# Layer 2's odd 96 rows: 32 rows of up beside gate, the other 64 as fp32 products, x joined by GpSimd

## The chip, the cores and the metric

The kernel runs on one core of one Trainium2 chip. The metric is the device time of one execution in microseconds (us). The engines are called PE (TensorE), DVE (VectorE), ACT (ScalarE), POOL (GpSimd) and SP (SyncE, which issues most DMAs).

## The reference

1024 tokens of width 512 go through two layers in fp32. Layer 1 is attention-like: a small Taylor expansion over 128 channels plus a feed-forward of width 1248, added to the input and layer-normalised. Layer 2, where the change lies, is a feed-forward with weights that are quantised and dequantised in the kernel:

```python
dq1 = nf4_quant_dequant(w1)      # 1376 x 512, blocks of 64 along a row
dq2 = nf4_quant_dequant(w2)      # 1376 x 512
dq3 = nf4_quant_dequant(w3)      # 512 x 1376
gate = jnp.einsum('bsd,hd->bsh', x, dq1)
up = jnp.einsum('bsd,hd->bsh', x, dq2)
h = jax.nn.silu(gate) * up
return jnp.einsum('bsh,dh->bsd', h, dq3)
```

The result is added to x and layer-normalised again. `nf4_quant_dequant` divides each block by its largest magnitude, takes the nearest of 16 codes and multiplies back.

## The kernel before

**Products.** Nearly every fp32 operand is split into a high part and a low part of type fp32r, and a product is three matmuls (`product`, L1294 to L1297): high by high, high by low, low by high. x is in `x_hi` and `x_lo`, a weight chunk in one of two slots of `w_hi` and `w_lo`, a half of h in one of four slots of `l_hi` and `l_lo`.

**Layer 2, first stage.** w1 and w2 (gate and up) are taken 128 rows at a time, as eleven units (0 to 10); 1376 is ten times 128 and 96, so the last one, unit 10, has 96 rows of each. A pair is one unit with one half of the tokens (512): gate in one PSUM bank, up in the next, twelve matmuls of 512 columns for each (`pair`, L1337, `project`, L1307). There are 22 pairs, 0 to 21, on banks 0, 1 and 2, 3 in turn; pairs 20 and 21 are the odd ones. After a pair ACT writes silu of gate to h and copies up to `up2` (L682, L690), and POOL multiplies the two (L1257). A pair waits until ACT has copied the up of the pair but one before it; the copy waits for POOL's product of the pair but one before that.

**Layer 1's odd rows.** Layer 1's first chunk (pairs 0 and 1 there) has 96 rows too, and is already worked in another way: gate's 96 rows and 32 of up share one set of 128 columns of weights, and the other 64 rows of up are eight fp32 matmuls, not split, four for each token half, on 64 columns of weights (`project_up`, L1328 to L1335). They write rows 0 to 63 and 64 to 127 of one bank.

**Quantising.** Units 0 to 10 lie in `Q`; units 11 to 16 are w3, two chunks of it each (the last: one). A unit is worked in eight steps. Before them DVE takes the block maxima and POOL divides by them (L1211, by reciprocals). At step k (1 to 7; step 0 has no level) ACT draws a line into an int8 tile `side` (L599 from L640; step 0 is L637), POOL clamps it to a `level` (L1220), DVE adds it up in PSUM (L887; for k=1 L883, which reads `side` and `level`, both in SBUF). After step 7 DVE multiplies the maxima back (L890). I write 15.4 for step 4 of unit 15. There are four `side` and three `level` buffers. At 10.3 DVE also works out the scales of all of w3 (L868 to L872), for which ACT exchanges partners' maxima before 10.2; POOL's division of unit 11 comes before 10.5 and needs them.

**From a quantised unit to weights.** DVE transposes a unit into PSUM banks 4 and 5 (L1030), ACT copies the high part (`split_nf4`), DVE subtracts to get the low part (`lo_nf4`, L1039). A unit's first pair waits for both. Stage two (h by w3, jobs of twelve matmuls) does the same with chunks of w3 (L1047, L729, L1055), and its first job waits for chunk 0's low part.

**The order of the work** is written out: each engine runs its main list in order, and calls `beside()` ahead of each item, which does as many quantising steps as the next number of that engine's list in `SHARE` says (L222). Nothing on an engine overtakes what stands ahead of it. Around the places that matter the lists before read (main items by name, gate n for POOL's product of pair n):

```
POOL: 9.1 9.2 9.3 | gate 1 | gate 2 | 9.4 9.5 | gate 3 | 9.6 9.7 10.0 10.1 | gate 4 | 10.2 | gate 5 | 10.3 10.4 10.5 | gate 6 | 10.6 10.7 11.0 11.1 | gate 7 | 11.2 11.3 | gate 8
POOL: 15.0 to 15.3 | gate 19 | 15.4 15.5 | gate 20
DVE:  10.2 | low part of unit 4 | 10.3 | transpose of unit 5 | 10.4 to 11.1 | low part of unit 5
DVE:  14.7 15.0 to 15.4 | low part of w3 chunk 0 | transpose of chunk 2 | 15.5 | low part of chunk 1
```

Of the kernel before, what the change touches and what calls it, by code (L numbers as in the profile page):

```python
# [29 lines left out]
P = 128  # L30
# [11 lines left out]


REST, LEFT = F1 % P, 64
assert 2 * REST - P == LEFT
KEEP_FROM = 5
PRE0 = 2 * P

# [79 lines left out]

def unit_width(u):
    if u < C2:  # L130
        return 2 * DC * min(P, F2 - u * P)
    return D * min(2, C2 - 2 * (u - C2))


def w3_unit_of(c):
# [78 lines left out]
def multiplied(i, pool):  # L214
# [8 lines left out]
    "scalar": [  # L223
# [6 lines left out]
    "vector": [  # L230
# [5 lines left out]
    "gpsimd": [  # L236
# [3 lines left out]
}  # L240


# [18 lines left out]
def build(nc, xT, xN, w_pre, w_fuse, w_in, w_out, consts, w12, w3, w3_end, ident_in, out):  # L261
    with ExitStack() as ctx:  # L262
# [41 lines left out]
        def turned(f):  # L304

            return PS[:, XT_BANK:XT_BANK + 2, :].rearrange("p b n -> p (b n)")[:, 0:unit_width(f)]

        def term_tile(m, a):
            return (up if m == 0 else odd_term if m % 2 else even_term)[:, a, :]

# [61 lines left out]
        s_st, s_ln, s_sqrt, s_norm = sem("s_st"), sem("s_ln"), sem("s_sqrt"), sem("s_norm")  # L372
        s_norm_last, s_quarter, s_mean = sem("s_norm_last"), sem("s_quarter"), sem("s_mean")
        s_centred, s_root = sem("s_centred"), sem("s_root")
        s_xtr, s_turn, s_w3turn = sem("s_xtr"), sem("s_turn"), sem("s_w3turn")
        s_max3, s_other, s_max3_all = sem("s_max3"), sem("s_other"), sem("s_max3_all")
        s_max, s_floor, s_prep, s_nrm = sem("s_max"), sem("s_floor"), sem("s_prep"), sem("s_nrm")
# [60 lines left out]
        def h_half(n):  # L438

            i, (kind, c) = SEQ[n]  # L440
            a, layer = i % 2, 1 if kind == "out" else 2
            view = h[0:job_rows(SEQ[n][1]), c * TOK + a * HALF:c * TOK + (a + 1) * HALF]
            return view, (s_h, 2 * c + a + 1) if layer == 1 else product_made(PAIR2[c, a])

        def product_made(i):

# [9 lines left out]
            return f, half, 2 * ((i + 2) % 3) if layer == 1 else 2 * (i % 2)  # L456


        UP_BANK = 5

        def parted_up(i):

            _, half, bank = pair_of(1, i)
            return [(slice(LEFT, REST), PS[REST:P, bank, :]),
                    (slice(0, LEFT), PS[half * LEFT:(half + 1) * LEFT, UP_BANK, :])]

        def h_of(layer, i):
            f, half, _ = pair_of(layer, i)
            p = rows1(f) if layer == 1 else rows(f, F2)
            return h[0:p, f * TOK + half * HALF:f * TOK + (half + 1) * HALF]  # L470

# [52 lines left out]
        def _(sp):  # L524
# [15 lines left out]
                sp.dma_start(w_raw(j)[0:p, 0:n], src).then_inc(s_raw[j % RAW_SLOTS], 16)  # L540

            def load_unit(u):
                sp.dma_start(unit_read(u), w12[:, u * UW:u * UW + unit_width(u)]).then_inc(s_q[u], 16)

            def load_residual(a):

# [50 lines left out]
        def _(act):  # L597
# [76 lines left out]
            def silu(layer, i):  # L674
                beside()
                act.wait_ge(s_pair, i + 1 + (2 * C1 if layer == 2 else 0))
                if layer == 2 and i == 0:

                    act.wait_ge(s_llo_h, 2 * C1)
                dst = h_of(layer, i)  # L680
                bank = pair_of(layer, i)[2]
                nc.scalar.activation(dst, PS[0:dst.shape[0], bank, :], ACT.Silu).then_inc(s_silu, 1)  # L682
                if layer == 2 and on_pool(i):
                    k = multiplied(i, True) - 1
                    if k == 0:
# [4 lines left out]
                    copy(up2[0:dst.shape[0], k % 2, :], PS[0:dst.shape[0], bank + 1, :]).then_inc(s_up2, 1)  # L690

            def root_of_variance(layer, g):
                beside()
# [21 lines left out]

            def split_nf4(f):
                beside()
                m = rows(f, F2)
                act.wait_ge(s_turn, f + 1)
                wait_nf4_slot(act, f)  # L720
                copy(in_slot(w_hi, f, 2 * DC * m), turned(f)).then_inc(s_whi4, 1)

            def split_w3(c):
                beside()
# [107 lines left out]
        def _(dve):  # L832
# [80 lines left out]
            def gate_times_up(layer, i):  # L913
                beside()
                dst = h_of(layer, i)
                dve.wait_ge(s_silu, i + 1 + (2 * C1 if layer == 2 else 0))
                if layer == 1 and i < 2:
                    for to, up_rows in parted_up(i):
# [113 lines left out]

            def lo_nf4(f):
                beside()
                m = rows(f, F2)
                n = 2 * DC * m
                dve.wait_ge(s_whi4, f + 1)
                wait_nf4_slot(dve, f)
                v.tensor_tensor(in_slot(w_lo, f, n), turned(f), in_slot(w_hi, f, n).bitcast(F32),  # L1039
                                ALU.subtract).then_inc(s_wlo4, 1)  # L1040

            def turn_w3(c):
                beside()
# [160 lines left out]
        def _(pool):  # L1204
# [37 lines left out]
            def lo_of_h(n):  # L1242
# [26 lines left out]
            for n in range(PASS_START[2]):  # L1269
# [21 lines left out]
        def _(pe):  # L1291
# [27 lines left out]
            def project_first(half, bank):  # L1319

                wh, wl = (in_slot(w, JOB["in", 0], DC * P).rearrange("p (c m) -> p c m", c=DC) for w in (w_hi, w_lo))
                for c in range(DC):
                    xs = slice(half * HALF, (half + 1) * HALF)
                    last = product(PS[:, bank, :], wh[:, c, :], wl[:, c, :], x_hi[:, c, xs], x_lo[:, c, xs], c == 0,
                                   c == DC - 1)
                return last

            def project_up():  # L1328

                w = w_raw(JOB["in", 0])[:, DC * P:2 * DC * REST].rearrange("p (c m) -> p c m", c=DC)  # L1330
                for c in range(DC):
                    for half in range(2):
                        last = t_.matmul(PS[half * LEFT:(half + 1) * LEFT, UP_BANK, :], w[:, c, :],  # L1333
                                         xT_raw[:, c, half * HALF:(half + 1) * HALF], start=c == 0, stop=c == DC - 1)
                return last  # L1335

            def pair(layer, i):  # L1337
                f, half, bank = pair_of(layer, i)
                m = rows1(f) if layer == 1 else rows(f, F2)
                if layer == 1:  # L1340
                    slot = JOB["in", f]
                    if half == 0:
# [8 lines left out]
                else:  # L1351
# [9 lines left out]
                if layer == 1 and i < 2:  # L1361
                    last = project_first(half, bank)
                    if half == 0:
                        last = project_up()
                    last.then_inc(s_pair, 1)
                    return
# [1 line left out]
                if (layer, i) == (2, 1):  # L1368
# [181 lines left out]
```

## Time and profile before

| | |
|---|---|
| median of 3 runs | 410.32 us (410.29 to 411.04) |
| the profiled execution | 410.1 us |
| its span, first to last instruction | 408.1 us |
| granted PE clock | 0.997 of 2.4 GHz |
| PE busy | 399.7 us, 98% of the span |
| DVE, ACT, POOL busy | 324.1, 266.9, 289.4 us |
| DMA | 26.42 MB, 18.8% of the DMA engines' time |

The time of an execution is the span and about 2 us around it. Busy time is summed over the instructions of an engine. A matmul's record is longer than its share of PE, since matmuls are pipelined: the distance from one start to the next is what it costs.

### The profile page before, as it was taken

Reading aid. Unit: us, or ns where it says so; the run is one execution under the profiler, and the core shown is the slowest. Engines: PE = TensorE matmul, PEld = TensorE weight load, DVE = VectorE, ACT = ScalarE, POOL = GpSimd, SP = SyncE. Lnnn points to the kernel's source line nnn. Section 1 sums busy time; section 2 is a strip of 40 time slices with the busy share of each in tenths; the row PEclk is TensorE's granted clock in tenths of the full one; section 3 lists DMA queues with packets and bytes.
Section 4 is the critical chain, followed back from the end, with each engine's and each line's share of the span. In section 5 each row is a group of like instructions: output and inputs, shape, how many; then the busy total and the mean of one; then the engine's idle time right before and its main releaser. Section 6 shows DMA issues by size and latency. Waiting matters only on the chain.

```text
span 408.1 us, 5343 instructions
## 1 busy us (share of the span) xinstructions
PE 399.7 (98%) x1762; PEld 326.0 (80%) x1762; DVE 324.1 (79%) x386; ACT 266.9 (65%) x372; POOL 289.4 (71%) x228
## 2 busy tenths in 40 slices
PE   8999999999999999999999999999999999999993
PEld 6767888888888888888888888888888877888872
DVE  4539889789789997999969799887789989926035
ACT  5574676686585837466955668887769777732613
POOL 0177998987977499737992465799999998954330
PEclk9999999999999999999999999999999999999998
DMA  8993101100103361003052000000000000000202
GB/s 269 405 408 135 53 22 50 28 26 0 53 26 104 101 214 65 27 0 104 1 177 102 0 2 0 0 2 0 2 2 0 2 0 0 2 1 0 104 0 103
DMA packets 10010, 26.42 MB, mean 65 GB/s; under 512 B 1248, under 2 KB 1632, under 8 KB 9728
## 3 DMA queue, kind: packets, MB, share of 16 engines
q1 hardware_dynamic: 9552, 25.30, 17.8%
q10 hardware_dynamic: 432, 0.79, 0.7%
q8 instruction: 14, 0.23, 0.2%
q14 instruction: 12, 0.10, 0.1%
HBM read 23.99 MB, written 2.10 MB: 64 GB/s over the span
## 4 chain that ended last, share of the span: by engine, by line
PE 95%; DVE 1%; POOL 1%; ACT 1%; issue 0%; POOLq 0%; DVEq 0%; ACTq 0%
PE PS L1295 31%; PE PS L1296 31%; PE PS L1297 31%; PE PS L1429 1%; PE PS L1333 1%; PE PS L1423 1%; POOL level L1220 1%; DVE h L919 0%; POOLq L262 0%; DVE PS L887 0%; PE PS L1438 0%; ACT side L637 0%; ACT side L599 0%; PE PS L1444 0%; PE PS L1441 0%
## 5 line engine op out<-in xcount | busy, mean ns | idle before, releaser
L1220 POOL TENSOR_SCALAR level<-side 128x1024 f32<-128x1024 int8 (+2 forms) x119 | 128.9, 1083 | 27.8 <-ACT side L599 15.5
L887 DVE TENSOR_TENSOR PS<-PS,level 128x1024 f32<-128x1024 f32 (+2 forms) x102 | 120.1, 1178 | 21.8 <-POOL level L1220 17.8
L1295 PE MATMUL PS<-x_hi,w_hi 128*128 128x512 f32 (+1 forms) x340 | 132.8, 391 | 0.3 <-DVE h L919 0.3
L1297 PE MATMUL PS<-x_hi,w_lo 128*128 128x512 f32 (+1 forms) x340 | 132.4, 390 | 0.0
L1296 PE MATMUL PS<-x_lo,w_hi 128*128 128x512 f32 (+1 forms) x340 | 132.4, 389 | 0.0
L599 ACT ACTIVATE side<-Q 128x1024 int8<-128x1024 f32 (+2 forms) x84 | 80.5, 998 | 21.5 <-DVE PS L883 17.8
L1250 POOL TENSOR_TENSOR l_lo<-h,l_hi 128x512 fp32r<-128x512 f32 (+1 forms) x42 | 57.3, 1373 | 26.5 <-ACT l_hi L599 25.8
L1295 PEld LDWEIGHTS PS<-x_hi,w_hi 128*128 128x128 f32 (+1 forms) x340 | 63.4, 187 | 15.2 <-issue 0.8
L1297 PEld LDWEIGHTS PS<-x_hi,w_lo 128*128 128x128 f32 (+1 forms) x340 | 63.4, 187 | 13.8
L1296 PEld LDWEIGHTS PS<-x_lo,w_hi 128*128 128x128 f32 (+1 forms) x340 | 63.4, 187 | 13.4
L1296 PE MATMUL PS<-x_lo,l_hi 128*128 128x512 f32 (+1 forms) x144 | 56.1, 389 | 0.0
L1295 PE MATMUL PS<-x_hi,l_hi 128*128 128x512 f32 (+1 forms) x144 | 56.1, 389 | 0.0
L1297 PE MATMUL PS<-x_hi,l_lo 128*128 128x512 f32 (+1 forms) x144 | 56.1, 389 | 0.0
L1239 POOL TENSOR_TENSOR w_lo<-raw,w_hi 128x1024 fp32r<-128x1024 f32 (+2 forms) x15 | 30.8, 2054 | 19.5 <-ACT w_hi L599 18.9
L682 ACT ACTIVATE h<-PS 128x512 f32<-128x512 f32 (+1 forms) x42 | 24.9, 593 | 29.6 <-PE PS L1297 26.4
L1257 POOL TENSOR_TENSOR h<-h,Q 128x512 f32<-128x512 f32 (+1 forms) x22 | 30.3, 1377 | 18.2 <-ACT Q L599 15.9
L599 ACT ACTIVATE l_hi<-h 128x512 fp32r<-128x512 f32 (+1 forms) x42 | 25.9, 626 | 25.3 <-PE PS L1297 25.3
L599 ACT ACTIVATE side<-raw 128x1024 int8<-128x1024 f32 x35 | 35.1, 1059 | 6.0 <-DVE PS L883 6.0
L1295 PE MATMUL PS<-w_hi,l_hi 128*128 128x512 f32 (+1 forms) x80 | 31.5, 394 | 0.2 <-POOL l_lo L1250 0.2
L1295 PEld LDWEIGHTS PS<-x_hi,l_hi 128*128 128x128 f32 (+1 forms) x144 | 27.0, 188 | 5.7
L1296 PEld LDWEIGHTS PS<-x_lo,l_hi 128*128 128x128 f32 (+1 forms) x144 | 27.0, 188 | 5.6
L1297 PEld LDWEIGHTS PS<-x_hi,l_lo 128*128 128x128 f32 (+1 forms) x144 | 27.0, 188 | 5.6
(104 smaller groups left out, 514.1 us busy)
## 6 DMA issues: line engine op xcount, KB each, us to landing
Q<-w SPq DMA_DIRECT2D x10, 512.0 KB, 13.8
raw<-w_in SPq DMA_DIRECT2D x9, 512.0 KB, 9.9
raw<-w_out SPq DMA_DIRECT2D x13, 256.0 KB, 2.8
raw<-w SPq DMA_DIRECT2D x5, 512.0 KB, 3.9
R<-xN SPq DMA_DIRECT2D x2, 1024.0 KB, 5.7
raw<-w_fuse SPq DMA_DIRECT2D x7, 256.0 KB, 2.6
out<-R SPq DMA_DIRECT2D x7, 256.0 KB, 2.0
h<-xT SPq DMA_DIRECT2D x2, 512.0 KB, 6.8
```

The source lines that it names most:

```text
L599: return nc.scalar.activation(dst, src, ACT.Copy, **kw)
L682: nc.scalar.activation(dst, PS[0:dst.shape[0], bank, :], ACT.Silu).then_inc(s_silu, 1)
L887: v.tensor_tensor(total, total, level_of(s), ALU.add).then_inc(s_add, 1)
L1220: g.tensor_scalar(level_of(s), side_of(s), LIMITS[k][1], LIMITS[k][0], ALU.min, ALU.max).then_inc(s_level, 1)
L1239: g.tensor_tensor(lo, w_raw(j)[0:p, 0:n], hi.bitcast(F32), ALU.subtract).then_inc(s_wlo_in if JOBS[j][0] == "in" else s_wlo, 1)
L1250: g.tensor_tensor(lo, view, hi.bitcast(F32), ALU.subtract).then_inc(s_llo_h, 1)
L1257: g.tensor_tensor(dst, dst, up2[0:dst.shape[0], k % 2, :], ALU.mult).then_inc(s_h2, 1)
L1295: t_.matmul(dst, a_hi, b_hi, start=start, stop=False)
L1296: t_.matmul(dst, a_hi, b_lo, start=False, stop=False)
L1297: return t_.matmul(dst, a_lo, b_hi, start=False, stop=stop)
L1333: last = t_.matmul(PS[half * LEFT:(half + 1) * LEFT, UP_BANK, :], w[:, c, :], xT_raw[:, c, half * HALF:(half + 1) * HALF], start=c == 0, s ...
L1423: last = t_.transpose(PS[:, XT_BANK + t % 2, c * P:(c + 1) * P], R[:, t, c * P:(c + 1) * P], ident[:])
```

## The change

The 96-row chunk of w1 and w2 moves from unit 10 to unit 4 (`ODD`), so pairs 8 and 9 are the odd ones; the other units keep 128 rows and their order (`CHUNK_OF`), and h keeps its place by chunk. In the odd pairs gate's 96 rows and up's last 32 form one set of 128 columns. Up's first 64 rows are copied by ACT out of PSUM as plain fp32 (`up2_raw`, into free columns of h), and multiplied as fp32 with `x2_raw`, which POOL makes from `x_hi + x_lo` in four additions of 128x1024 (`join_x`), ahead of its gates 2, 3, 4 and 5. These eight fp32 matmuls follow the split ones of pair 8, for both token halves, and write bank 1; pair 10, whose up goes to bank 1, also waits until ACT has copied the up of pair 9. ACT copies the up of an odd pair in two parts. The lists in `SHARE` are dealt anew from about unit 8's last steps on.

```diff
+ODD = 4
+CHUNK_OF = [*range(ODD), C2 - 1, *range(ODD, C2 - 1)]
 def unit_width(u):
     if u < C2:
-        return 2 * DC * min(P, F2 - u * P)
+        return 2 * DC * (REST if u == ODD else P)
...
+        x2_raw = h[:, 6 * TOK:(6 + DC) * TOK].rearrange("p (c t) -> p c t", c=DC)
+        up2_raw = h[:, 5 * TOK:5 * TOK + DC * LEFT].rearrange("p (s n) -> p s n", s=2)
...
+        UP_BANK = {1: 5, 2: 1}
...
+                    if is_odd(layer, i):
+                        for to, up_rows in parted_up(layer, i):
+                            last = copy(up2[to, k % 2, :], up_rows)
+                        last.then_inc(s_up2, 1)
...
+                if f == ODD:
+                    copy(up2_raw, odd_part(turned(f), 2 * P, 2 * (P + LEFT)))
+                    copy(odd_part(dst, 0, 2 * P), odd_part(turned(f), 0, 2 * P)).then_inc(s_whi4, 1)
...
+            def join_x(half, k):
+
+                pool.wait_ge(s_xl, X_PARTS + TILES * (half + 1))
+                x, hi, lo = (t[:, 2 * k:2 * k + 2, half * HALF:(half + 1) * HALF] for t in (x2_raw, x_hi, x_lo))
+                g.tensor_tensor(x, hi.bitcast(F32), lo.bitcast(F32), ALU.add).then_inc(s_x2raw, 1)
...
             for i in range(2 * C2):
+                if 2 <= i < 6:
+                    join_x(i // 2 - 1, i % 2)
                 if on_pool(i):
                     gate_times_up(i)
...
+            def project_up2():
+
+                w = up2_raw.rearrange("p s (k m) -> p k s m", k=2)
+                for c in range(DC):
+                    pe.wait_ge(s_x2raw, 3 + c // 2)
+                    for half in range(2):
+                        last = t_.matmul(PS[half * LEFT:(half + 1) * LEFT, UP_BANK[2], :], w[:, c // 2, c % 2, :],
+                                         x2_raw[:, c, half * HALF:(half + 1) * HALF], start=c == 0, stop=c == DC - 1)
                 return last
...
+                if is_odd(layer, i):
+                    last = project_odd(layer, slot, half, bank)
+                    if layer == 2 and half == 0:
+                        last = project_up2()
...
+                    if layer == 2 and i > 1 and is_odd(2, i - 2) and half == 0:
+
+                        pe.wait_ge(*bank_free(i - 1))
                     project(layer, slot, 1, half, bank + 1, m).then_inc(s_pair, 1)
```

Written out as above, the lists after read:

```
POOL: 9.1 9.2 9.3 | gate 1 | join | gate 2 | join | 9.4 to 9.7 | gate 3 | join | 10.0 10.1 | gate 4 | join | 10.2 10.3 | gate 5 | 10.4 10.5 10.6 | gate 6 | 10.7 | gate 7 | 11.0 to 11.3 | gate 8
POOL: 15.0 to 15.3 | gate 19 | 15.4 15.5 | gate 20
DVE:  9.7 10.0 to 10.3 | low part of unit 4 | 10.4 10.5 | transpose of unit 5 | 10.6 to 11.1 | low part of unit 5
DVE:  14.7 15.0 to 15.4 | low part of w3 chunk 0 | transpose of chunk 2 | low part of chunk 1 | transpose of chunk 3 | 15.5 | low part of chunk 2 | 15.6
```

## Rows read from the trace of the kernel before

**Rows 1.** The page: busy time by engine, and two rows of the 40 slices

```profile
PE 399.7 (98%) x1762; PEld 326.0 (80%) x1762; DVE 324.1 (79%) x386; ACT 266.9 (65%) x372; POOL 289.4 (71%) x228
...
PE   8999999999999999999999999999999999999993
...
POOL 0177998987977499737992465799999998954330
```

**Rows 2.** The page: the chain that ended last, by engine

```profile
PE 95%; DVE 1%; POOL 1%; ACT 1%; issue 0%; POOLq 0%; DVEq 0%; ACTq 0%
```

**Rows 3.** Timeline of PE: first matmul of pair 20, first of stage two

```profile
329.67 0.39 PE L1295 MATMUL PS<-x_hi,w_hi 128*96 128x512 f32 x1
...
340.75 0.39 PE L1295 MATMUL PS<-w_hi,l_hi 128*128 128x512 f32 x1
```

**Rows 4.** Timeline of ACT: silu after pairs 7 and 8, high parts of w3

```profile
264.59 0.60 ACT L682 ACTIVATE h<-PS 128x512 f32<-128x512 f32 x1 [0.79 <-PE PS L1297]
...
270.03 0.60 ACT L682 ACTIVATE h<-PS 128x512 f32<-128x512 f32 x1 [1.55 <-PE PS L1297]
...
336.38 1.08 ACT L599 ACTIVATE w_hi<-PS 128x512 fp32r<-128x512 f32 x2
```

**Rows 5.** The chain in order of time: layer 1's eight fp32 matmuls (16 records)

```profile
19.79 3.61 PE PS L1333 x16
```

**Rows 6.** Busy time in stretches; columns PE, PEld, DVE, ACT, POOL, then clock, DMA

```profile
235.60:260.00 24.40, 24.40 (x109) 20.24 (x108) 23.85 (x23) 19.70 (x34) 14.41 (x14) 1.00 0.00 1
260.00:336.00 76.00, 76.00 (x337) 62.13 (x336) 64.07 (x56) 59.20 (x77) 71.69 (x58) 1.00 0.00 1
```

**Rows 7.** Timeline of POOL, 238 to 272 us: start, us, what, [idle before]

```profile
238.61 1.30 POOL L1257 TENSOR_TENSOR h<-h,Q 128x512 f32<-128x512 f32 x1 [3.01 <-ACT Q L599]
240.41 1.04 POOL L1220 TENSOR_SCALAR level<-side 128x1024 f32<-128x1024 int8 x1 [0.50 <-ACT side L599]
241.54 1.47 POOL L1211 TENSOR_TENSOR Q<-Q,rcp 128x768 f32<-128x768 f32 x1
...
253.20 0.83 POOL L1220 TENSOR_SCALAR level<-side 128x768 f32<-128x768 int8 x1 [2.07 <-ACT side L599]
...
259.74 1.92 POOL L1211 TENSOR_TENSOR raw<-raw,Q 128x1024 f32<-128x1024 f32 x1 [1.48 <-DVE Q L872]
...
268.35 3.03 POOL L1220 TENSOR_SCALAR level<-side 128x1024 f32<-128x1024 int8 x2
```

**Rows 8.** Timeline of POOL in layer 1: subtractions of 128x1024

```profile
65.47 3.37 POOL L1239 TENSOR_TENSOR w_lo<-raw,w_hi 128x1024 fp32r<-128x1024 f32 x1
...
74.02 2.40 POOL L1239 TENSOR_TENSOR w_lo<-raw,w_hi 128x1024 fp32r<-128x1024 f32 x1
```

**Rows 9.** Timeline of DVE: additions that read two SBUF tiles

```profile
65.37 1.22 DVE L883 SCALAR_TENSOR_TENSOR PS<-side,level 128x1024 f32<-128x1024 int8 x1
...
235.94 1.22 DVE L883 SCALAR_TENSOR_TENSOR PS<-side,level 128x1024 f32<-128x1024 int8 x1
...
253.21 1.63 DVE L883 SCALAR_TENSOR_TENSOR PS<-side,level 128x768 f32<-128x768 int8 x1
```

**Rows 10.** Timeline of DVE: unit 4's low part, the scales of w3

```profile
254.94 0.97 DVE L887 TENSOR_TENSOR PS<-PS,level 128x768 f32<-128x768 f32 x1
255.82 1.21 DVE L1039 TENSOR_TENSOR w_lo<-PS,w_hi 128x1024 fp32r<-128x1024 f32 x1
256.95 0.59 DVE L868 TENSOR_TENSOR Q<-Q 128x176 f32<-128x176 f32 x1
...
258.40 1.25 DVE L872 RECIPROCAL Q<-Q 128x176 f32<-128x176 f32 x1
```

**Rows 11.** Timeline of POOL: the level of step 15.4

```profile
334.82 1.04 POOL L1220 TENSOR_SCALAR level<-side 128x1024 f32<-128x1024 int8 x1
```

**Rows 12.** Timeline of DVE: step 15.4, then w3 chunk 0's low part

```profile
335.89 1.23 DVE L887 TENSOR_TENSOR PS<-PS,level 128x1024 f32<-128x1024 f32 x1 [0.76 <-POOL level L1220]
337.04 0.68 DVE L1055 TENSOR_TENSOR w_lo<-PS,w_hi 128x512 fp32r<-128x512 f32 x1
```

More of the change, by code:

```diff
@@ L44 @@
 REST, LEFT = F1 % P, 64
-assert 2 * REST - P == LEFT
+assert F2 % P == REST and 2 * REST - P == LEFT
+ODD = 4
+CHUNK_OF = [*range(ODD), C2 - 1, *range(ODD, C2 - 1)]
 KEEP_FROM = 5
@@ L442, in h_half @@
             view = h[0:job_rows(SEQ[n][1]), c * TOK + a * HALF:c * TOK + (a + 1) * HALF]
-            return view, (s_h, 2 * c + a + 1) if layer == 1 else product_made(PAIR2[c, a])
+            return view, (s_h, 2 * c + a + 1) if layer == 1 else product_made(PAIR2[CHUNK_OF.index(c), a])
         def product_made(i):
@@ L456, in pair_of, with is_odd, parted_up @@
             return f, half, 2 * ((i + 2) % 3) if layer == 1 else 2 * (i % 2)
-        UP_BANK = 5
-        def parted_up(i):
-            _, half, bank = pair_of(1, i)
+        UP_BANK = {1: 5, 2: 1}
+        def is_odd(layer, i):
+            return pair_of(layer, i)[0] == (0 if layer == 1 else ODD)
+        def parted_up(layer, i):
+            _, half, bank = pair_of(layer, i)
             return [(slice(LEFT, REST), PS[REST:P, bank, :]),
-                    (slice(0, LEFT), PS[half * LEFT:(half + 1) * LEFT, UP_BANK, :])]
+                    (slice(0, LEFT), PS[half * LEFT:(half + 1) * LEFT, UP_BANK[layer], :])]
         def h_of(layer, i):
             f, half, _ = pair_of(layer, i)
+            if layer == 2:
+                f = CHUNK_OF[f]
             p = rows1(f) if layer == 1 else rows(f, F2)
@@ L689, in silu @@
                         act.wait_ge(s_h2, k - 1)
-                    copy(up2[0:dst.shape[0], k % 2, :], PS[0:dst.shape[0], bank + 1, :]).then_inc(s_up2, 1)
+                    if is_odd(layer, i):
+                        for to, up_rows in parted_up(layer, i):
+                            last = copy(up2[to, k % 2, :], up_rows)
+                        last.then_inc(s_up2, 1)
+                    else:
+                        copy(up2[0:dst.shape[0], k % 2, :], PS[0:dst.shape[0], bank + 1, :]).then_inc(s_up2, 1)
             def root_of_variance(layer, g):
@@ L717, in split_nf4 @@
                 beside()
-                m = rows(f, F2)
                 act.wait_ge(s_turn, f + 1)
                 wait_nf4_slot(act, f)
-                copy(in_slot(w_hi, f, 2 * DC * m), turned(f)).then_inc(s_whi4, 1)
+                dst = in_slot(w_hi, f, unit_width(f))
+                if f == ODD:
+                    copy(up2_raw, odd_part(turned(f), 2 * P, 2 * (P + LEFT)))
+                    copy(odd_part(dst, 0, 2 * P), odd_part(turned(f), 0, 2 * P)).then_inc(s_whi4, 1)
+                else:
+                    copy(dst, turned(f)).then_inc(s_whi4, 1)
             def split_w3(c):
@@ L916, in gate_times_up @@
                 dve.wait_ge(s_silu, i + 1 + (2 * C1 if layer == 2 else 0))
-                if layer == 1 and i < 2:
-                    for to, up_rows in parted_up(i):
+                if is_odd(layer, i):
+                    for to, up_rows in parted_up(layer, i):
                         last = v.tensor_tensor(dst[to, :], up_rows, dst[to, :], ALU.mult)
@@ L1034, in lo_nf4 @@
                 beside()
-                m = rows(f, F2)
-                n = 2 * DC * m
                 dve.wait_ge(s_whi4, f + 1)
                 wait_nf4_slot(dve, f)
-                v.tensor_tensor(in_slot(w_lo, f, n), turned(f), in_slot(w_hi, f, n).bitcast(F32),
-                                ALU.subtract).then_inc(s_wlo4, 1)
+                hi, lo = (in_slot(w, f, unit_width(f)) for w in (w_hi, w_lo))
+                if f == ODD:
+                    hi, lo, src = (odd_part(x, 0, 2 * P) for x in (hi, lo, turned(f)))
+                else:
+                    src = turned(f)
+                v.tensor_tensor(lo, src, hi.bitcast(F32), ALU.subtract).then_inc(s_wlo4, 1)
             def turn_w3(c):
@@ L1317, in project, with project_odd @@
                 return last
-            def project_first(half, bank):
-                wh, wl = (in_slot(w, JOB["in", 0], DC * P).rearrange("p (c m) -> p c m", c=DC) for w in (w_hi, w_lo))
+            def project_odd(layer, slot, half, bank):
+                if layer == 1:
+                    parts = (in_slot(w, slot, DC * P) for w in (w_hi, w_lo))
+                    wh, wl = (w.rearrange("p (c m) -> p c m", c=DC) for w in parts)
+                else:
+                    parts = (in_slot(w, slot, unit_width(ODD)) for w in (w_hi, w_lo))
+                    wh, wl = (odd_part(w, 0, 2 * P).rearrange("p s (k m) -> p k s m", k=2) for w in parts)
                 for c in range(DC):
+                    w_h, w_l = ((w[:, c, :] if layer == 1 else w[:, c // 2, c % 2, :]) for w in (wh, wl))
                     xs = slice(half * HALF, (half + 1) * HALF)
-                    last = product(PS[:, bank, :], wh[:, c, :], wl[:, c, :], x_hi[:, c, xs], x_lo[:, c, xs], c == 0,
-                                   c == DC - 1)
+                    last = product(PS[:, bank, :], w_h, w_l, x_hi[:, c, xs], x_lo[:, c, xs], c == 0, c == DC - 1)
+                return last
+            def project_up2():
[5 more added lines that the diff above has]
+                                         x2_raw[:, c, half * HALF:(half + 1) * HALF], start=c == 0, stop=c == DC - 1)
                 return last
@@ L1332, in project_up @@
                     for half in range(2):
-                        last = t_.matmul(PS[half * LEFT:(half + 1) * LEFT, UP_BANK, :], w[:, c, :],
+                        last = t_.matmul(PS[half * LEFT:(half + 1) * LEFT, UP_BANK[1], :], w[:, c, :],
                                          xT_raw[:, c, half * HALF:(half + 1) * HALF], start=c == 0, stop=c == DC - 1)
@@ L1338, in pair @@
                 f, half, bank = pair_of(layer, i)
-                m = rows1(f) if layer == 1 else rows(f, F2)
+                m = P
                 if layer == 1:
@@ L1360, in pair @@
                     pe.wait_ge(s_xl, X_PARTS + (TILES if half == 0 and i < 2 else TT))
-                if layer == 1 and i < 2:
-                    last = project_first(half, bank)
-                    if half == 0:
+                if is_odd(layer, i):
+                    last = project_odd(layer, slot, half, bank)
+                    if layer == 2 and half == 0:
+                        last = project_up2()
+                    elif half == 0:
                         last = project_up()
@@ L1512, in by_squares @@
         parts = []
-        for f in range(C2):
+        for f in CHUNK_OF:
             rows_ = [w[f * P:(f + 1) * P].reshape(-1, SQ, 2, DC, BLOCK) for w in ws]
+            if f == C2 - 1:
+                gate, up = rows_
+                parts += [x.transpose(3, 1, 2, 0, 4).reshape(P, -1)
+                          for x in (np.concatenate([gate, up[LEFT // SQ:]]), up[:LEFT // SQ])]
+                continue
             parts.append(np.stack(rows_).transpose(4, 2, 0, 3, 1, 5).reshape(P, -1))
```

7 lines of the change are left out of this document (6 added, 1 removed), and 16 rows, old and new, of the table SHARE.

## The prediction

> **What bounds the kernel now.** I read the page first: PE is busy 98% of the span and nearly every slice of its row is 9, while POOL, at 71% over all, stands at 9 in nearly all slices of layer 2's first stage [rows 1]. The chain that ended last is 95% PE [rows 2]. So what shortens PE's own work shortens the run, as long as no other engine comes late. The reader is to see two things: where PE's work shrinks, and which engine behind it has the least to spare. Timelines of PE and ACT give PE's prices [rows 3, 4], the chain in order of time that of the fp32 matmuls [rows 5]; the stretches and timelines behind them [rows 6 to 12] are about POOL and DVE, because it is the engine to which the change gives work, in the very stage where it is full: between 260 and 336 us it is busy 71.69 of 76.00 us, and its 58 instructions leave the rest as gaps of under 0.1 us [rows 6].
>
> **PE.** Pairs 20 and 21, the 96-row ones, take from 329.67 to 340.75, 11.08 us for 48 matmuls [rows 3]: a set of 96 columns costs no less than one of 128. A pair of full width takes 5.44 us, the distance of ACT's silus after pairs 7 and 8 [rows 4], so 24 matmuls cost 5.44 us. The odd pairs become 24 such matmuls and eight fp32 ones. Those were already run in layer 1, with the same shape: 3.61 us [rows 5]. New cost 5.44 + 3.61 = 9.05 us, gain 2.03 us. That is the most that the change can bring, for PE does nothing else less.
>
> The Trainium skill ("FP8 and Floating Point Precision", TensorE Precision Notes) says that a true fp32 matmul takes four passes through the array. The row shows less than that rule would give one after the other: 3.61 us is 16 times 0.226 us for eight matmuls, two passes' worth each. By the page's four the change would lose on PE; that is a rival below.
>
> **POOL, the price.** Four joins of 128x1024 with two full fp32 operands. No join is in the trace; the same form, the subtraction of a split at that size, takes 2.40 us alone [rows 8], the division of a unit, whose second operand is one number a block, 1.92 [rows 7]. The bounds are 1.9 and 3.4, the 3.37 us being the case that collides (below). I take 2.4, as both operands are full: 9.7 us with the gaps. Unit 10 is now 1024 wide instead of 768: seven levels at 1.04 instead of 0.83 and a division at 1.92 instead of 1.47 [rows 7] are 1.9 us. Unit 4 is cheaper by as much, but its steps lie far ahead, and POOL later waits for gate 0 anyway, so nothing comes back.
>
> Third, collisions. Where DVE's step 1 (L883), which reads two SBUF tiles, started just ahead of a POOL instruction, at 65.37 us, that one took 3.37 us instead of 2.40 [rows 8, 9]. At 253.21 DVE's took 1.63 us, for POOL had begun at 253.20 a level of 0.83 us and DVE's addition went on only after it [rows 7, 9]. One holds the other off. In the kernel before, the two such additions at 235.94 and 253.21 [rows 9] met a POOL that was about to be idle and cost it nothing. Now the first falls into a join, ends near 239.2 and takes 0.6 us from gate 2; the second reaches into the fourth join and takes 1.0. That is 1.6 us. From unit 11 on the collisions are in the rows already.
>
> **POOL, the cover.** From 235.60 to 260.00 it is busy 14.41 of 24.40 us [rows 6]; less the gaps between 14 instructions, 9.4 us are idle, 3.01 of them ahead of gate 2, 2.07 and 1.48 near the end [rows 7]. The joins fall there. About 0.8 us stays idle: from the first join's end, 238.0, to gate 2, which ACT's copy holds to 238.6, and 0.2 before unit 11 is divided. So POOL falls behind by 9.7 + 1.9 + 1.6 + 0.8 - 9.4 = **4.6 us**. Behind 260 us there is no gap to catch up in [rows 6], and up to step 15.4 both kernels have the same steps, gates and subtractions on POOL.
>
> **Where it meets PE.** Four places, in order.
> - Unit 4's low part now stands behind 10.3 on DVE, and 10.3 behind the scales of w3. By my working the fourth join ends at 258.9 and the level of 10.2 at 260.0; its addition ends at 261.2, the scales take 2.7 (256.95 to 259.65) [rows 10], 10.3 another 1.1, the low part of 512 columns 0.7: 265.7. PE wants it at the end of pair 7, 264.6 [rows 4]. Before, it followed 10.2 at 255.82 [rows 10], over 7 us ahead. PE waits 1.1 us.
> - Unit 5's low part stands behind the level of 11.1, which now comes behind gate 7, at 272.9: ready at 275.3, wanted at 264.6 + 1.1 + 9.05 = 274.8. PE waits 0.5 us. From 275.3, twelve pairs at 5.44 end at 340.6, just before the 340.75 of before: these two waits alone eat most of the gain.
> - Units 6 to 10: before, their low parts came 5 us and more ahead of their pairs; POOL being 4.6 late and PE about level, they are close but in time.
> - Chunk 0 of w3. Its low part is behind 15.4 on DVE. The level of 15.4 ended at 335.86 [rows 11] and DVE had waited 0.76 us for it; the low part ended at 337.72 [rows 12], with ACT's high part done by then [rows 4], 3.0 us before PE wanted it [rows 3]. Now it ends at 337.72 + 4.6 = **342.3**, and stage two starts there: 342.3 - 340.75 = 1.6 us later than before.
>
> Behind that point: DVE needs about 1.8 us a chunk of w3 and PE 2.7, and unit 16 is small, so PE finds each chunk ready, if by little; I add nothing.
>
> **Costed at nothing, and why.** ACT's split of unit 4 in two copies and the second copies for the odd pairs (about 0.6 us each): ACT has 59.20 busy in 76 us [rows 6]. The wait of pair 10 on pair 9's copy: silu and two copies are 1.8 us, and the twelve gate matmuls of pair 10 ahead of the wait take 2.7; if ACT is held by a level, up to 1 us of it could show, and then the matmuls of up, nothing else, stand behind it. PE's wait for the joins: the last ends at 258.9, the fp32 matmuls come after 268. SP's queue moves nothing; the loads are the same bytes, long before.
>
> **Sum.** The profiled execution took 410.1 us: 410.1 + 1.6 = 411.7. The median shown is 0.2 above it, so 411.9 us.
>
> **Rivals.** What a measurement of this kernel can tell from no change is about 0.2%, 0.8 us.
> - *POOL late by 2.4 to 3.9 us only.* The collisions cost nothing (DVE gives way, or meets the idle that is left): 4.6 - 1.6 = 3.0, chunk 0 at 340.7, and PE's own path about there too: 410.3. For it: each collision depends on a few tenths. Against it: the two seen [rows 8, 9]. 27%.
> - *The joins are covered: faster.* If a join costs as little as the division, 1.92, and collides with nothing, POOL gets 7.7 + 1.9 against 9.4 of idle time, and is late by under 1 us. Below 1.0 us late, chunk 0 is ready by 338.7, where PE now arrives; then all of 2.03 us stays: 408.3. It decides at that one point, DVE's step 15.4. For it: 9.4 us of idle time stand in the very stretch where the joins are issued [rows 6]. Against it: 2.40 for the same form [rows 8]. 20%.
> - *The fp32 matmuls take twice as long here.* 7.2 us instead of 3.6: pair 10 starts 3.6 later, stage two at about 344, 413.5. Against it: the same shape in layer 1 [rows 5]. 4%.
> - *More waits than I see* (ACT held up by late gates and so late with lines, which makes POOL idle): 413 and over. 4%.
>
> My forecast has 45%: POOL late by 4.0 to 5.7 us, 411.2 to 413.0. The change not doing what it says is excluded as a rival: the 24 matmuls are gone from the code.
>
> **The numbers.** 411.9 us. The range takes in the middle rival, most of the faster one's partial cases (a gain of up to 1.6 us) and the slower ones to 413.4: 408.7 to 413.4. Faster by over 0.2%: 0.21, the covered case and a little. Within 0.2%: 0.28. Slower: 0.51, the forecast and the last two.
>
> **What would show it.** In the changed profile: eight fp32 matmuls in 3.6 us inside pair 8; joins of 2.4 us, one of them over 3; POOL without idle from 240 us on; gate 7 ending near 271.8; the level of 15.4 near 340.5; PE idle a little before pairs 8 and 10, and 1 to 2 us before the first matmul of stage two, put down to DVE. Wrong if joins take under 2 us, if POOL still shows idle time of some us before 260, or if stage two starts by 339.5.

## The result and the profile after

The changed kernel takes 412.17 us (median of 7 runs, 411.33 to 412.48), the kernel before 410.56 us in the same comparison: ratio 1.0032, 95% interval 1.0022 to 1.0042. It is slower by 1.6 us, as forecast (1.6 us on 410.3).

The page of the changed kernel, busy time, three rows of the slices and the chain:

```profile
span 410.5 us, 5334 instructions
...
PE 399.4 (97%) x1754; PEld 323.5 (79%) x1754; DVE 326.2 (79%) x386; ACT 267.8 (65%) x375; POOL 300.1 (73%) x232
...
PE   8999999999999999999999999899999999999993
...
POOL 0077998987876499737992599999999999874430
...
PE 93%; DMA 2%; DVE 1%; issue 1%; ACT 1%; POOL 1%; POOLq 0%; SPq 0%; DVEq 0%; ACTq 0%
```

POOL has 10.7 us more work than before [rows 1], and its row is full from the slice of 236 us on; PE's row has an 8 where it had nines. The chain has a DMA of the start in it: in this execution the first x came later, and everything up to layer 2 is 0.86 us later than before (ACT's silu of pair 2 starts at 238.25 instead of 237.39). In the profiled executions of this study, e5 and e6 apart, that silu lay from 0.2 us earlier to 1.4 us later than before, so times in layer 2 are compared after taking this shift off ("aligned"). That is also why the profiled execution, 412.5 us, is 2.4 us above the one of before and the medians are 1.6 apart.

The timeline of PE in the changed kernel: the start of pair 8, its fp32 matmuls, the start of pair 10 and of stage two. "issue" is a wait for which the view has no releaser; the low parts below end just ahead of them.

```profile
266.55 0.47 PE L1336 MATMUL PS<-x_hi,w_hi 128*128 128x512 f32 x1 [1.06 <-issue]
...
269.49 3.65 PE L1380 MATMUL PS<-h 128*64 128x512 f32 x16
...
277.28 0.47 PE L1336 MATMUL PS<-x_hi,w_hi 128*128 128x512 f32 x1 [1.19 <-issue]
...
343.12 0.47 PE L1336 MATMUL PS<-w_hi,l_hi 128*128 128x512 f32 x1 [0.26 <-issue]
```

Stage two starts at 343.12, aligned 342.26, 1.51 us after the 340.75 of before [rows 3]; I had put 1.6. PE stood idle only 0.4 us ahead of it, not the 1 to 2 us that I had named as a sign; the rest of the loss lies in the two waits before.

POOL's timeline: the joins are L1289, gate 2 is the L1296 at 239.48, the last row is the level of 15.4.

```profile
236.48 2.40 POOL L1289 TENSOR_TENSOR h<-x_hi,x_lo 128x1024 f32<-128x1024 f32 x1
239.48 1.64 POOL L1296 TENSOR_TENSOR h<-h,Q 128x512 f32<-128x512 f32 x1 [0.60 <-ACT Q L621]
241.07 2.41 POOL L1289 TENSOR_TENSOR h<-x_hi,x_lo 128x1024 f32<-128x1024 f32 x1
...
256.17 3.39 POOL L1289 TENSOR_TENSOR h<-x_hi,x_lo 128x1024 f32<-128x1024 f32 x1
...
340.12 1.04 POOL L1253 TENSOR_SCALAR level<-side 128x1024 f32<-128x1024 int8 x1
```

DVE's timeline: the two collisions with joins (L914, which was L883), the low parts of units 4 and 5 (L1073), 15.4 and chunk 0 of w3.

```profile
236.79 3.17 DVE L914 SCALAR_TENSOR_TENSOR PS<-side,level 128x1024 f32<-128x1024 int8 x1
...
255.66 1.65 DVE L914 SCALAR_TENSOR_TENSOR PS<-side,level 128x1024 f32<-128x1024 int8 x1
...
260.72 1.23 DVE L918 TENSOR_TENSOR PS<-PS,level 128x1024 f32<-128x1024 f32 x1 [3.42 <-POOL level L1253]
...
265.77 0.68 DVE L1073 TENSOR_TENSOR w_lo<-PS,w_hi 128x512 fp32r<-128x512 f32 x1
...
274.12 1.92 DVE L914 SCALAR_TENSOR_TENSOR PS<-side,level 128x1024 f32<-128x1024 int8 x1
275.96 1.21 DVE L1073 TENSOR_TENSOR w_lo<-PS,w_hi 128x1024 fp32r<-128x1024 f32 x1
...
341.20 1.23 DVE L918 TENSOR_TENSOR PS<-PS,level 128x1024 f32<-128x1024 f32 x1 [0.76 <-POOL level L1253]
342.34 0.68 DVE L1088 TENSOR_TENSOR w_lo<-PS,w_hi 128x512 fp32r<-128x512 f32 x1
```

The reader sees the whole mechanism here: DVE held by a join (3.17 us instead of 1.22), a join by DVE (3.39 instead of 2.40), 10.2's addition waiting 3.42 us for its level behind a join, and each low part ending just before PE's next start.

### The profile page after: what moved, and what is told of

It reads as the page before. It is cut to its first block, busy times and chain, and to the rows that moved or that the text cites. A ratio compares the mean times of both kernels' runs of the same rounds, so it can differ in the third digit from the quotient of the medians.

```text
span 410.5 us, 5334 instructions
## 1 busy us (share of the span) xinstructions
PE 399.4 (97%) x1754; PEld 323.5 (79%) x1754; DVE 326.2 (79%) x386; ACT 267.8 (65%) x375; POOL 300.1 (73%) x232
## 4 chain that ended last, share of the span: by engine, by line
PE 93%; DMA 2%; DVE 1%; issue 1%; ACT 1%; POOL 1%; POOLq 0%; SPq 0%; DVEq 0%; ACTq 0%
PE PS L1336 30%; PE PS L1337 30%; PE PS L1338 30%; DMA h<-xT 2%; PE PS L1389 1%; PE PS L1380 1%; PE PS L1484 1%; POOL level L1253 1%; DVE h L950 0%; POOLq L269 0%; DVE PS L918 0%; ACT side L659 0%; ACT side L621 0%; SPq L576 0%; ACT R L621 0%
## 5 line engine op out<-in xcount | busy, mean ns | idle before, releaser
L1336 PE MATMUL PS<-x_hi,w_hi 128*128 128x512 f32 x332 | 130.0, 392 | 2.7 <-issue 2.2
L1338 PE MATMUL PS<-x_hi,w_lo 128*128 128x512 f32 x332 | 129.3, 389 | 0.0
L1337 PE MATMUL PS<-x_lo,w_hi 128*128 128x512 f32 x332 | 129.2, 389 | 0.0
L1336 PEld LDWEIGHTS PS<-x_hi,w_hi 128*128 128x128 f32 x332 | 62.3, 188 | 19.1 <-issue 5.4
L1338 PEld LDWEIGHTS PS<-x_hi,w_lo 128*128 128x128 f32 x332 | 62.3, 188 | 13.1
L1337 PEld LDWEIGHTS PS<-x_lo,w_hi 128*128 128x128 f32 x332 | 62.3, 188 | 12.5
L1296 POOL TENSOR_TENSOR h<-h,Q 128x512 f32<-128x512 f32 (+1 forms) x22 | 29.8, 1356 | 14.6 <-ACT Q L621 13.1
```

The source lines that it names most:

```text
L1336: t_.matmul(dst, a_hi, b_hi, start=start, stop=False)
L1337: t_.matmul(dst, a_hi, b_lo, start=False, stop=False)
L1338: return t_.matmul(dst, a_lo, b_hi, start=False, stop=stop)
```

## The experiments

Ratios are to the kernel before, whose median lay between 410.4 and 410.7 us in these comparisons.

| run | median, us | ratio, 95% interval |
|---|---|---|
| e1, no joins | 408.75 | 0.9957 (0.9943 to 0.9970) |
| e2, two fp32 matmuls | 412.98 | 1.0058 (1.0038 to 1.0078) |
| e3, before with joins | 411.60 | 1.0027 (1.0017 to 1.0037) |
| e4, w3 first | 411.50 | 1.0027 (1.0017 to 1.0036) |
| e5, all joins early | 411.26 | 1.0014 (1.0005 to 1.0023) |
| e6, half of them early | 411.67 | 1.0029 (1.0018 to 1.0039) |
| e7, units 4 and 5 first | 415.83 | 1.0120 (1.0104 to 1.0136) |
| e8, these and w3 first | 415.41 | 1.0115 (1.0100 to 1.0130) |
| e9, joins behind the normalisation | 409.07 | 0.9966 (0.9953 to 0.9979) |
| e10, that and w3 first | 408.49 | 0.9957 (0.9943 to 0.9971) |
| e11, unit 4 first | 415.24 | 1.0107 (1.0090 to 1.0123) |

**e1: no joins.** In the changed kernel:

```diff
-                if 2 <= i < 6:
-                    join_x(i // 2 - 1, i % 2)
...
-                    pe.wait_ge(s_x2raw, 3 + c // 2)
...
-                                         x2_raw[:, c, half * HALF:(half + 1) * HALF], start=c == 0, stop=c == DC - 1)
+                                         x_hi[:, c, half * HALF:(half + 1) * HALF].bitcast(F32), start=c == 0, stop=c == DC - 1)
```

> The changed kernel without the four joins; the fp32 products read the high part of x alone, so the low part of x is left out of up's 64 rows. My theory (POOL falls behind by the joins and the collisions, and with it the low parts that PE waits for): POOL has only unit 10's extra 1.9 us, which 9.4 us of idle time cover; PE waits at pairs 8 and 10 and before stage two vanish, and PE's own saving of 1.7 to 2.0 us shows: 1.7 us below the kernel before (408.8 against 410.5). Rival (the new order on DVE, low parts behind the scales of w3 and behind more levels, makes them late, joins or not): still at or above the kernel before. Rival (the joins are only half of it): between, 0.5 us below to 0.5 above.

1.8 us below the kernel before. PE stands still at none of the three places; its timeline there, and POOL's level of 15.4:

```profile
267.30 0.39 PE L1336 MATMUL PS<-x_hi,w_lo 128*128 128x512 f32 x1
267.62 0.65 PE L1377 MATMUL PS<-x_hi,h 128*64 128x512 f32 x2
...
339.38 0.47 PE L1334 MATMUL PS<-w_hi,l_hi 128*128 128x512 f32 x1
```

```profile
336.38 1.05 POOL L1253 TENSOR_SCALAR level<-side 128x1024 f32<-128x1024 int8 x1
```

Stage two starts at 339.38, aligned 338.96, 1.8 us before that of before. The joins are the loss, all of it, and DVE's new order harms nothing without them. But POOL is not on time even here: the level of 15.4 ends at 337.43, aligned 337.0, 1.2 us later than before, where I had expected the idle time to cover all. At unit 11's division (260.62, aligned 260.2) it is 0.5 us late [rows 7], and at 273.29 it stood 0.5 us more ahead of a gate, for ACT. Chunk 0's low part ended at 339.28, just in time.

**e2: less work for PE.** Two fp32 matmuls instead of eight: `for c in range(DC)` is `for c in range(1)` in `project_up2`, with `start=True, stop=True`.

> The changed kernel with two fp32 matmuls instead of eight (three of the four parts of the sum over x are left out of up's 64 rows): 2.7 us of PE's work less. My theory: pair 10 waits for unit 5's low part, which POOL and DVE set at 277.2 us; pair 10 starts no earlier, and the time stays that of the changed kernel, 1.3 to 1.6 us above the kernel before; the idle time before pair 10 grows from 1.4 to about 4 us. Rival (PE's own work sets the end): 2.7 us less than the changed kernel, 1.1 us below the kernel before.

No gain from 2.7 us less of work. Pair 10 started at 277.89, aligned 276.5, as in the changed kernel (276.4), behind an idle time of 4.0 us; so the low part of unit 5 sets it. The time was even 0.8 us above the changed kernel's, for a reason that I had not expected. PE's timeline, and two stretches (the column behind the busy times is the granted clock):

```profile
277.89 0.47 PE L1336 MATMUL PS<-x_hi,w_hi 128*128 128x512 f32 x1 [3.81 <-DVE w_lo L1073]
...
280.74 0.63 PE L1336 MATMUL PS<-x_hi,w_hi 128*128 128x512 f32 x1
281.17 0.63 PE L1337 MATMUL PS<-x_lo,w_hi 128*128 128x512 f32 x1
```

```profile
280.00:285.00 5.00, 5.00 (x18) 4.01 (x17) 3.30 (x4) 3.83 (x5) 4.67 (x5) 0.74 0.00 0
285.00:290.00 5.00, 5.00 (x23) 4.13 (x23) 4.76 (x5) 4.76 (x7) 4.76 (x5) 1.00 0.00 0
```

From 279.5 to 282.5 us matmuls follow each other by 0.43 us instead of 0.23, and the granted clock of the stretch is 0.74: the lower level, 1.2 GHz. Some seven of them cost about 1.4 us. The one of six executions of this kernel with a mean clock of 0.998 took 411.5 us, the five with 0.987 to 0.992 took 412.6 to 414.3.

**e3: the joins alone.** The four `join_x` calls and their semaphore added to the kernel before, nothing else.

> The kernel before with the four joins alone added on POOL at the same places, their result unused. My theory: POOL falls behind by 9.7 + 1.6 + 0.8 - 9.4 = 2.7 us, the level of 15.4 ends at 338.6 instead of 335.9 and chunk 0's low part at 340.4, still 0.3 us ahead of PE: no change, within 0.3 us of the kernel before. Rival (the joins disturb PE by themselves, by reading x beside it): slower by 1 us or more, with longer matmuls. Rival (the collisions cost more than I take): slower by 0.5 us, with a wait before stage two.

1.0 us slower, where I had expected nothing. The mechanism is the one I had, its size and its reach are not. POOL's level of 15.4, and PE's second wait in stage two:

```profile
338.20 1.04 POOL L1223 TENSOR_SCALAR level<-side 128x1024 f32<-128x1024 int8 x1
```

```profile
343.33 0.50 PE L1306 MATMUL PS<-w_hi,l_hi 128*128 128x512 f32 x1 [0.50 <-ACT Q L602]
```

POOL is 3.4 us late (339.24 against 335.86 [rows 11]), not 2.7: the 1.48 us ahead of unit 11's division were not filled, 1.3 us more than I took, while the collisions took 0.8 us (gate 2 1.49 instead of 1.30, a level 1.42 instead of 0.83), not 1.6. Chunk 0's low part ended at 341.10; PE started stage two at 341.20, and then stood 0.7 us more, not for a low part but for ACT's copy of the last pair's up. That copy stands behind quantising lines on ACT, the first of which had waited 2.24 us for DVE, and DVE for POOL. PE also lost 0.2 us before one earlier matmul, at 313.60. No matmul was longer than before, so the joins don't disturb PE.

**e4: chunk 0 of w3 ahead of 15.4 on DVE.** Two numbers of DVE's list in `SHARE`, 6, 0 to 5, 1.

> The changed kernel with w3 chunk 0's low part ahead of step 15.4 on DVE, instead of behind it. In the changed kernel's trace the waits before pairs 8 and 10 alone bring PE to 342.7, and chunk 0's low part holds it to 343.1. My theory as now read: 0.4 us less than the changed kernel, 1.2 us above the kernel before. Rival (chunk 0's low part is what sets the time, as I had put it): 1.2 us less or more, level with the kernel before. A third: 15.4 and what follows it come later, and a later chunk waits: no gain.

Stage two at 342.16, aligned 341.82, 0.4 us earlier than in the changed kernel. The medians are 0.7 us apart, the ratios 0.2, and the intervals of the ratios overlap, so the size rests on the trace. By it chunk 0 was the last 0.4 us of the loss, and PE's own path, with the waits before pairs 8 and 10, set the rest.

**e5: all joins early.** In the changed kernel:

```diff
             def gate_times_up(i):
                 beside()
+                if i == 0:
+                    join_x(0, 0)
+                    join_x(0, 1)
...
-                if 2 <= i < 6:
-                    join_x(i // 2 - 1, i % 2)
+                if 2 <= i < 4:
+                    join_x(1, i % 2)
```

> The changed kernel with the joins at other places on POOL and nothing else: the two of the first token half just ahead of gate 0's wait, where POOL stands idle for 12.5 us, the two of the second half ahead of gates 2 and 3. My theory: two joins cost POOL nothing, the other two, unit 10's 1.9 us and one collision of 0.6 are 7.3 us against 9.4 us of idle time, so POOL is late by under 1 us; no wait before pairs 8 and 10 and stage two; 1.7 us below the kernel before, as without any join. Rival (a join costs by reading x beside PE, or the order of DVE's list costs): at least 0.7 us above that, at or over the kernel before.

0.6 us above the kernel before: wrong by 2.3 us. The waits before pairs 8 and 10 are gone. But earlier, two joins run at 218.07 to 222.83 us beside DVE's steps of layer 1's normalisation. POOL's and DVE's timelines:

```profile
218.07 4.76 POOL L1289 TENSOR_TENSOR h<-x_hi,x_lo 128x1024 f32<-128x1024 f32 x2
```

```profile
218.89 1.60 DVE L1015 TENSOR_SCALAR std<-mv 128x2 f32<-128x2 f32 x1
220.41 1.22 DVE L918 TENSOR_TENSOR PS<-PS,level 128x1024 f32<-128x1024 f32 x1
221.54 0.15 DVE L1018 RECIPROCAL std<-std 128x2 f32<-128x2 f32 x1
221.72 1.13 DVE L1019 TENSOR_TENSOR std<-std 128x2 f32<-128x2 f32 x1
```

In the changed kernel L1015 and L1019 take 0.17 and 0.16 us. Here each, on two elements a partition, ends with the join beside it (220.5 and 222.8). The two between them, an addition that has one operand in PSUM and a reciprocal, take their usual time beside the second join. The steps stand between PE and its next x, and PE waits twice:

```profile
230.55 1.23 PE L1487 MATMUL PS<-ident,R 128*128 128x128 f32 x8 [0.77 <-DVE x_lo L1049]
...
234.42 0.47 PE L1339 MATMUL PS<-x_hi,w_hi 128*128 128x512 f32 x1 [0.57 <-DVE x_lo L1049]
```

ACT's silu of pair 2 comes at 240.18, 1.9 us later than before once the 0.9 us are taken off by which it was already late at 216 us, ahead of the joins; with 0.3 us of wait ahead of stage two this is nearly all of the 2.3 us.

**e6: half of the joins early.** As e5, with the second token half's joins left ahead of gates 4 and 5.

> As the run before, but with the joins of the second token half left where the change has them, ahead of gates 4 and 5. My theory: 4.9 us of joins, 1.9 of unit 10 and a collision of 1.0 against the 6.4 us of idle time behind gate 2, of which some 1 us stays unfilled: POOL late by 2 us or a little more, half of the changed kernel's; between the two, 0.5 to 1.2 us below the kernel before. Rival (only the number of joins counts, not the idle time they fall in): the time of the changed kernel.

1.0 us above. It pays the same price in the normalisation (1.49 and 1.13 us for the same two operations) and keeps 0.6 us of wait before pair 10 and 0.4 before stage two. It says nothing against the theory, but it can't be read as support either; e5 and e9 do what it was meant to do.

**e7: units 4 and 5 ahead of levels on DVE.** In DVE's list 5, 2, 4, 0, 4 is now 4, 3, 2, 0, 6 (low part 4, transpose 5, low part 5, transpose 6, low part 6).

> The changed kernel with DVE's list put so that unit 4's low part comes ahead of step 10.3 and the scales of w3, and unit 5's ahead of steps 11.0 and 11.1. Both waits of PE there, 1.2 and 1.3 us, go. My theory: POOL is as late as before, so later low parts (unit 8's, w3 chunk 0's at 342) hold PE instead: 0.1 to 0.5 us less than the changed kernel. Rival (the waits before pairs 8 and 10 are the loss, POOL's lateness behind them is harmless): 2.5 us less than the changed kernel, 0.9 us below the kernel before.

5.1 us slower than before: my edit made a new wait. It put DVE's 11.1 behind unit 5's low part; ACT's line of 11.4 needs that addition, and ACT's copy of pair 9's up stands behind the line. That is the copy for which pair 10 now waits, on bank 1. ACT, then PE's two waits in pair 10, for unit 5's low part and on bank 1:

```profile
279.37 1.06 ACT L622 ACTIVATE side<-raw 128x1024 int8<-128x1024 f32 x1 [3.21 <-DVE PS L915]
```

```profile
275.93 0.47 PE L1337 MATMUL PS<-x_hi,w_hi 128*128 128x512 f32 x1 [1.48 <-DVE w_lo L1074]
...
282.18 0.50 PE L1337 MATMUL PS<-x_hi,w_hi 128*128 128x512 f32 x1 [3.25 <-ACT Q L622]
```

The wait that the change adds costs nothing where it is, and 3.4 us once ACT is held. The wait before pair 8 is gone, but that for unit 5's low part is still there, 1.6 us. The run doesn't test what it was made for. Part of the 5.1 us is the clock: the execution shown took 414.3 us at a mean clock of 0.998, the other four 415.6 to 416.3 at 0.990 to 0.994.

**e8: e7 and e4 together.**

> The run before and w3 chunk 0's low part ahead of step 15.4 as well. My theory: units 4 and 5 and chunk 0 are on time; unit 8's low part, behind 13.1, and ACT's copies, held behind lines that wait for POOL, are what is left: 0.8 to 1.5 us less than the changed kernel, level with the kernel before to 0.8 us above it. Rival (POOL's lateness costs only through these three low parts): 1.7 us below the kernel before, as without joins.

The same wait, 3.23 us, and 4.7 us slower than before. On the low parts nothing follows beyond e7. On the clock something does: PE stood idle equally long, 3.4 us, in both profiled executions, and behind it seven matmuls follow each other by 0.43 us here (282.6 to 285.6 us) and none in e7. The stretch from 280 to 285 us, e7 first, then e8:

```profile
280.00:285.00 5.00, 2.82 (x12) 2.35 (x13) 3.40 (x4) 4.94 (x8) 4.67 (x5) 1.00 0.00 0
```

```profile
280.00:285.00 5.00, 2.98 (x8) 2.38 (x9) 3.41 (x4) 4.94 (x8) 4.67 (x5) 0.75 0.00 0
```

**e9: the early joins behind the normalisation.** As e5, and one more wait ahead of the first two joins:

```diff
                 if i == 0:
+                    pool.wait_ge(s_shift, len(NORM_GROUPS))
                     join_x(0, 0)
```

> As the run with all joins early, but the two ahead of gate 0 also wait until DVE has finished layer 1's last normalisation (224.5 us), so that they run from there to 229.5. In the early run two small DVE operations of that normalisation, on 128x2 elements, took 1.60 and 1.13 us instead of 0.17 and 0.16 while a join ran on POOL, and PE waited 0.9 and 0.7 us for x. My theory: a POOL join holds off DVE, which hurts only where DVE is on PE's path; those 1.7 us come back and the rest of the early run's gain shows: 1.2 to 1.6 us below the kernel before. Rival (the joins held PE or ACT up, or the early run was slow for another reason): the time of the early run, 0.5 us above the kernel before.

1.3 us below the kernel before, 2.2 us below e5, with the same joins 6.6 us later. Its POOL and PE:

```profile
224.68 4.76 POOL L1289 TENSOR_TENSOR h<-x_hi,x_lo 128x1024 f32<-128x1024 f32 x2 [7.52 <-DVE std L1022]
229.66 1.30 POOL L1300 TENSOR_TENSOR h<-h,Q 128x512 f32<-128x512 f32 x1 [0.22 <-ACT Q L621]
```

```profile
339.31 0.47 PE L1340 MATMUL PS<-w_hi,l_hi 128*128 128x512 f32 x1
```

Both joins fit between the normalisation and gate 0, and PE doesn't wait before stage two but for 0.3 us.

**e10: e9 and e4 together.**

> The run before and, on DVE, w3 chunk 0's low part ahead of step 15.4. The early run still showed a wait of 0.3 us before stage two. My theory: that wait goes, 0.2 to 0.4 us less than the run before, so 1.5 to 1.9 us below the kernel before, near the time without any join. Rival (what follows 15.4 becomes late instead): no gain on the run before.

408.49 us, 1.9 us below the kernel before and 3.7 below the changed one (3.1 by the ratios): all of the saving on PE, with all of the work. Stage two starts at 338.86, aligned 339.06, 0.3 us earlier than in e9. That it beats e9 is not shown by the times: the ratios are 0.4 us apart and their intervals overlap.

**e11: unit 4 ahead of 10.3 only.** In DVE's list 5, 2 is 4, 3.

> The changed kernel with unit 4's low part ahead of step 10.3 and the scales of w3, and nothing else moved. My theory: the wait before pair 8 goes, but unit 5's low part comes when POOL and DVE let it, so pair 10 waits that much longer, 2.5 us instead of 1.3: the time of the changed kernel within 0.3 us, plus up to 1 us if PE's granted clock falls behind the longer idle time, as it did behind 4 us of it. Rival (each wait costs by itself): 1.2 us less than the changed kernel.

The wait before pair 8 went, as expected, and nothing was gained, as expected; but it is 3.1 us above the changed kernel, more than I allowed. PE's timeline and one stretch:

```profile
278.84 0.47 PE L1337 MATMUL PS<-x_hi,w_hi 128*128 128x512 f32 x1 [3.53 <-DVE w_lo L1074]
```

```profile
280.00:285.00 5.00, 5.00 (x18) 3.98 (x17) 3.68 (x4) 4.79 (x6) 4.75 (x4) 0.73 0.00 0
```

Pair 10 starts at 278.84, aligned 277.4, 1.0 us later than in the changed kernel (the scales of w3 come later on DVE, and with them unit 11's division). The two waits of 1.2 and 1.3 us have become one of 3.7, and behind it the clock falls again, for seven matmuls: 1.4 us. Against this stands the 0.4 us of wait ahead of stage two, which is gone; stage two starts 2.2 us later, aligned. The other 0.6 us between the two profiled executions (415.24 and 412.48) come from ahead of pair 2 (shifts of 1.43 and 0.86 us). The medians differ by 0.3 us more, since the changed kernel's profiled execution lies that much above its median.

## Why the prediction was right, point by point

- **PE's saving, 2.03 us.** The odd pairs took 9.4 us, not 9.05: 2.94 for the first twelve matmuls, 3.58 for the fp32 ones, 2.86 for the last. So 1.7 us. The fp32 matmuls cost what layer 1's do [rows 5]; what was missed is about 0.1 us at each change between kinds and after a wait. The size didn't enter the result, since pair 10 hung on unit 5's low part (e2). Four passes one after the other, the rival's 7.2 us, are ruled out: sixteen records in 3.6 us. Whether a matmul here takes fewer passes, or those on the two halves of the columns overlap, no run shows.
- **A join, 2.4 us.** 2.40 alone, 3.39 in collision [rows 8]. Right.
- **The collisions, 1.6 us.** 0.3 on gate 2 and 1.0 on the fourth join. Right but for 0.3.
- **POOL late by 4.6 us.** The level of 15.4 ends at 341.16, aligned 340.3: 4.4 us late [rows 11]. Right as a total, the parts less so. By e1, 3.3 us of it come from the joins and their collisions, by e3, 3.4 us; the rest is there without joins (e1: 0.5 us at unit 11's division, 1.2 at 15.4). My sum had POOL on time without joins, since it set 1.9 us of work against all 9.4 us of idle time.
- **Unit 4.** Its low part ended at aligned 265.6; I had 265.7. PE waited 1.2 us.
- **Unit 5.** Aligned 276.3; I had 275.3, so PE waited 1.3 instead of 0.5 us. The step that failed: I let DVE's addition of 11.1 start when its level was there, aligned 273.0 as I had put it (272.9), and take 1.2 us. DVE was still multiplying unit 10's maxima back (L921), 0.3 us; by then POOL had begun the next level, and the addition took 1.92 us, held off by it, 0.7 us: a collision in the other direction, which I had seen in the rows but costed only for POOL. It is not the joins' doing: without them (e1) the same addition takes 1.93 us.
- **Chunk 0 of w3 sets the time.** It ended at aligned 342.2, as I said (342.3). But PE's own path, 340.6 in my sum, was at 341.8 (e4), nearly all through unit 5's low part. So the loss of 1.5 us was set by the waits before pairs 8 and 10 up to its last 0.4 us, not by chunk 0 from 340.6 on. The number stood because both paths end near each other: e4 takes only the last part off, e11 only moves the first wait into the second. The total was right by the path that I had named; the share between the two paths was not, and that it didn't matter was luck: 0.5 us more on unit 5 and PE's own path would have set the time.
- **Units 6 to 10, close but in time.** PE waits for none of them. Right.
- **The wait on bank 1, at nothing.** No wait in the changed kernel. e7 shows that it is 3.4 us when ACT is held, more than the 1 us I allowed.
- **The rivals.** "The joins are covered" fell in this kernel and came true in e9 and e10, by place and not by a cheaper join. Its point of decision, DVE's 15.4, was a good one only as the last of three. "POOL late by 2.4 to 3.9 us only" fell with 4.4, the doubled fp32 matmuls with 3.6 us. "More waits than I see", from ACT held up, did not come in this kernel but in e3 and e7.

Left open: e6's own question, and whether e10 is faster than e9.

## What to carry to other kernels

Where an engine is full for a long stretch, sum its work and its idle time from the last point at which it was idle. The difference arrives undiminished later (in e3 POOL is 3.4 us late at unit 11's division and 3.4 at 15.4, 75 us behind it), and the slack of each item that hangs on it (3.0 and 5 us here) says who pays. A saving on the bounding engine that is paid with work elsewhere is worth what that work finds free; the same four additions cost 3.4 us where the change has them (e1 against it) and 0.3 to 0.5 us in e9, by where they stood. Idle time is not one sum to draw on, either: without joins POOL had 9.4 us of it for 1.9 us of work, and was 0.5 us late all the same. Before moving work into an idle gap, ask what the neighbour engine does there: a gap beside a serial chain of small operations is not free.

## What the runs showed of the hardware that I had not expected

- While POOL ran a 2.4 us addition of two SBUF tiles, DVE operations on 128x2 elements took 1.60 and 1.13 us instead of 0.17 and 0.16, a `TENSOR_SCALAR` with one tensor source among them; a reciprocal between them took its usual 0.15 us. The Trainium skill ("GPSIMD Engine Reference", Specifications) says that GpSimd's SBUF interfaces are shared with VectorE, with contention for operations in a 2-port mode or with two SBUF inputs; the trace agrees for the second: the operations with two SBUF inputs that are shown were held until POOL's instruction ended (a small one 1.13 us instead of 0.16; in the changed kernel an addition 3.17 us instead of 1.22), while one of 128x1024 with one input in PSUM took its usual 1.22 us beside a join. In which mode the `TENSOR_SCALAR` ran the trace doesn't show.
- After PE had stood idle for 3.4 to 4.0 us, its granted clock fell to 1.2 GHz for about 3 us, 0.6 to 1.6 us behind the restart (e2, e8, e11), which cost 1.4 us. It did not always: in e7's profiled execution it stayed at 1.00 behind 3.4 us, and one of e2's six executions had a mean clock of 0.998. After the idle times of 1.2 and 1.3 us in the changed kernel it stayed at 1.00. A long wait can cost more than its own length.
